# A mixture-of-experts stage: expert sums as 64-token transposes on two half arrays, gate temporaries in SBUF, and a later order of preparation

## The chip, the cores and the metric

The kernel runs on one core of one Trainium2 chip. The metric is the device time of one execution in microseconds (us); the median of three runs is 1518.93 us (1518.44 to 1519.48).

## The reference

The input has shape 16 x 64 x 36 x 100 (batch, channels, height, width), float32. Cut to what matters:

```python
x = x + conv(ln_c(x), w_d, w_u, w_r, w_l)       # four recurrent sweeps: down, up, right, left
t = to_tokens(x)                                # 57600 tokens of 64 channels
probs = softmax(ln_t(t) @ router_w + router_b)  # 8 experts
top_p, top_i = top_k(probs, 2); top_p /= sum(top_p)
expert_out = einsum('bnd,edc->bnec', ln_t(t), expert_w) + expert_b
t = t + einsum('bnk,bnkc->bnc', top_p, take(expert_out, top_i))
```

So every token goes through all eight 64 x 64 experts, and the gate, which is zero for six of them, weights the eight results before they are summed.

## The kernel before

The program has three stages: the vertical sweeps, row by row; the horizontal sweeps, column by column; and, from about 920 us on, the feed-forward stage, which is all that the change touches. In that stage the image lies in SBUF as 18 regions `j` of 128 partitions x 1600 positions (two image rows share the partitions, 64 channels each). A region is cut into 13 tiles `p` of 128 positions, the last of 64, and a tile's two halves `q` (the two image rows) are 2 x 128 tokens. Tiles are taken three at a time as five chunks `c` for the preparation.

While a region's experts run, the next region is prepared between them. Every engine has its instructions in an order written out by hand in its own `region` function, loop over `p`:

- TensorE (PE): `experts(p)`, six matmuls of 512 columns in two halves of 64 rows, the tile's tokens against all experts into one of two twin banks; `tokens(c)`, centring and router logits (L977); `channels(c)`, transposes back (L991); `sum_experts(p-2)`, four accumulating transposes of a 128 x 128 block (L1022), which add the eight weighted results and turn them into the image's layout.
- VectorE (DVE): `gate_tile(p)` (L793) weights the experts' results, both halves of a tile (1024 elements) or one half (512); `square_sums` (L725), `second_part` (L733), the 17 steps of the gate's softmax and top two (L749 to L765, at places that `STEP_AT` names as (tile, part)), and `add_out` (L801), which adds the sums of four tiles to the image.
- ScalarE (ACT): `gate_odd(p)` (L506) weights the other half of the tiles in `ACT_TILES`, eight instructions each; `copy_tokens` (L473, L474), `inv_std_tokens` (L481, L483), `first_part` (L491).
- GpSimd (POOL): `pair_sums(p)` (L322) adds experts 4 to 7 to experts 0 to 3, so that four blocks are left; `scale_tokens(c)` (L335, L336) at tiles 2 to 6, ahead of that tile's pair sums.

`experts(p)` waits until both gate engines are through with tile p-2. `channels(c)` waits for `second_part(c-1)`, since both use bank 5. The sum of a group of four tiles waits until `add_out` has read the group before from bank 7 (`SUM`). Softmax step 0 waits for the last `scale_tokens` of the region, later steps each for the one before. Its temporaries `work` and `small` and the bias row lie in PSUM bank 6 (`LOG`).

Of the kernel before, what the change touches and what calls it, by code (L numbers as in the profile page):

```python
# [12 lines left out]
def metaformer_kernel(nc, x, x_col, w_d, w_u, w_r, w_l, router_w, router_b, expert_w, expert_b, out):  # L13
# [13 lines left out]
    TN = 128  # L27
# [10 lines left out]
    with ctx:  # L38
# [69 lines left out]
        CEN0, VAR0 = [2, 3, 6, 7], [4, 5]  # L108
        FRONT = CH + 2
        CT, TB = 4, 5  # L110
        LOG, SUM = 6, 7
        PREP = [6, 7]
        FILL_CT, FILL_TB = [4, 0, 1, 2, 3], [5, 7, 5, 7, 5]

        ACT_TILES = (2, 4, 5, 6, 7, 8, 9, 10)
        TERMS = [(0, 0), (0, 1), (1, 0)]
        LAG = 2
        SEQ = 2 * TILES
# [4 lines left out]

            return len(ACT_TILES) * j + sum(a <= p for a in ACT_TILES)

        bias_row = banks[LOG][:, 2 * NSM + 3 * NG:2 * NSM + 3 * NG + E]

        def stage_of(k):

# [16 lines left out]
        def later(n):  # L146
# [5 lines left out]
        GAP_STEP = 8  # L152
        EX_STEP = 12

        STEP_AT = [(7, 0), (7, 1), (7, 2), (8, 0), (8, 1), (8, 2), (9, 0), (9, 1), (9, 2), (10, 0), (10, 1), (10, 2),
                   (11, 0), (11, 1), (11, 2), (12, 0), (12, 1)]
        EXP_TILE = STEP_AT[GAP_STEP - 1][0] + 1

# [196 lines left out]
        def _(act):  # L355
# [109 lines left out]
            def copy_tokens(j, slot, c, bank=CT):  # L465
                n, b, k = NCK * j + c, (slot + c) % 2, len(tiles_of(c))
                src = banks[bank][:, 0:TC * CLW].rearrange("p (t n) -> p t n", t=TC)[:, 0:k]
                act.wait_ge(s_ct, n + 1)
                if later(n - 1):
                    act.wait_ge(s_vr, n - 1)  # L470
                if later(j):
                    act.wait_ge(s_tb, n - NCK + 1)
                act.activation(sqt[:, b, 0:k], src[:, :, 0:P], ACT.Square).then_inc(s_sq2, 1)  # L473
                act.activation(tl[:, c, 0:k], src, ACT.Copy).then_inc(s_cp, 1)  # L474

            def inv_std_tokens(j, slot, c):
                n, b, k = NCK * j + c, (slot + c) % 2, len(tiles_of(c))
                act.wait_ge(s_vr, n + 1)
                if later(n - 1):
                    act.wait_ge(s_xn2, n - 1)  # L480
                act.activation(stat[:, 1, b, 0:2 * k], stat[:, 0, b, 0:2 * k], ACT.Ln, bias=eps_c[:, 1:2], scale=1.0 / C).then_inc(s_ln2, 1)  # L481
                act.wait_ge(s_ln2, n + 1)
                act.activation(stat[:, 2, b, 0:2 * k], stat[:, 1, b, 0:2 * k], ACT.Exp, scale=-0.5).then_inc(s_r2, 1)  # L483

            def first_part(j, slot, c, bank=TB):

                n, k = NCK * j + c, len(tiles_of(c))
                act.wait_ge(s_tb, n + 1)
                if c == 0 and later(j - 1):
                    act.wait_ge(s_p, TILES * (j - 1))  # L490
                act.activation(tok[:, slot, 0, TC * TN * c:TC * TN * c + TN * k], banks[bank][:, 0:TN * k],  # L491
                               ACT.Identity, bias=1.0).then_inc(s_th, 1)
# [17 lines left out]
            def region(j, slot, now):  # L510

                for p in range(TILES):
                    if now is not None:
                        if p == EXP_TILE:
                            exponential(now)
                        if 2 <= p < NCK + 2:
                            inv_std_tokens(now, 1 - slot, p - 2)
                    if p in ACT_TILES:
                        gate_odd(j, slot, p)
                    if now is not None:  # L520
                        if p < NCK:
                            copy_tokens(now, 1 - slot, p)
                        if 3 <= p < NCK + 3:
                            first_part(now, 1 - slot, p - 3)

            for c in range(NCK + 2):
                if c < NCK:
# [15 lines left out]
        def _(dve):  # L543
# [96 lines left out]
            for q in range(2):  # L640
                half = slice(q * C, (q + 1) * C)
                nc.vector.tensor_copy(cl_w[half, P + q * E:P + (q + 1) * E], ew[half, E * C:]).then_inc(s_em, 1)
            nc.vector.tensor_copy(bias_row, eb[:, E * C:]).then_inc(s_em, 1)
            dve.wait_ge(s_em, 8)
            nc.vector.tensor_tensor(em[:, 1], ew[:, 0:E * C], em[:, 0].bitcast(F32), ALU.subtract).then_inc(s_em, 1)
            with dve.Fori(1, (HP - 2) // 2) as i:
# [70 lines left out]
            def flat(j):  # L717
                return cols[:, j].rearrange("p g w b -> p (g w b)")
# [18 lines left out]
                return v.unsqueeze(2).to_broadcast([P, NG, E])  # L737

            gap, ex, inv = (best[:, k] for k in range(3))
            work = banks[LOG][:, 0:2 * NSM].rearrange("p (k n e) -> p k n e", k=2, e=E)  # L740
            small = banks[LOG][:, 2 * NSM:2 * NSM + 3 * NG].rearrange("p (k n) -> p k n", k=3)
            m1, idx, den = (small[:, k] for k in range(3))

            def softmax_steps(j, slot):


                v = nc.vector
                return [
                    lambda: v.tensor_tensor(logit, raw_logit, bias_row.unsqueeze(1).to_broadcast([P, NG, E]), ALU.add),  # L749
                    lambda: v.tensor_reduce(m1, logit, AX.X, ALU.max),  # L750
                    lambda: v.tensor_tensor(work[:, 0], logit, spread(m1), ALU.subtract),
                    lambda: v.scalar_tensor_tensor(hit, work[:, 0], 0.0, rank_w[:, :, :], ALU.is_equal, ALU.mult),
                    lambda: v.tensor_reduce(idx, hit, AX.X, ALU.max),
                    lambda: v.tensor_tensor(first, rank_w[:, :, :], spread(idx), ALU.is_equal),
                    lambda: v.scalar_tensor_tensor(work[:, 1], first, -BIG, work[:, 0], ALU.mult, ALU.add),
                    lambda: v.tensor_reduce(gap, work[:, 1], AX.X, ALU.max),
                    lambda: v.tensor_tensor(work[:, 1], work[:, 1], spread(gap), ALU.subtract),
                    lambda: v.scalar_tensor_tensor(hit, work[:, 1], 0.0, rank_w[:, :, :], ALU.is_equal, ALU.mult),
                    lambda: v.tensor_reduce(idx, hit, AX.X, ALU.max),
                    lambda: v.tensor_tensor(work[:, 0], rank_w[:, :, :], spread(idx), ALU.is_equal),  # L760
                    lambda: v.tensor_scalar(den, ex, 1.0, None, ALU.add),
                    lambda: v.reciprocal(inv, den),
                    lambda: v.tensor_tensor(work[:, 1], work[:, 0], spread(ex), ALU.mult),
                    lambda: v.tensor_tensor(work[:, 0], work[:, 1], first, ALU.add),
                    lambda: v.tensor_tensor(gate[slot], work[:, 0], spread(inv), ALU.mult),  # L765
                ]
# [28 lines left out]
            def add_out(j, g):  # L795

                lo, hi = g * QUAD, min((g + 1) * QUAD, TILES)
                width, off = (QUAD * TN, 0) if hi < TILES else (TAIL, TN - TAIL)
                dst = flat(j)[:, lo * TN:lo * TN + width]
                dve.wait_ge(s_y, TILES * j + hi)  # L800
                nc.vector.tensor_tensor(dst, banks[SUM][:, off:off + width], dst, ALU.add).then_inc(s_o, 1)  # L801

            def add_behind(j, p):

# [7 lines left out]
            def region(j, slot, now):  # L812

                for p in range(TILES):
                    for part in range(3):
                        if part == 0:
                            gate_tile(j, slot, p)
                            if now is not None:
                                if 1 <= p < NCK + 1:
                                    square_sums(now, 1 - slot, p - 1)  # L820
                                if 4 <= p < NCK + 4:
                                    second_part(now, 1 - slot, p - 4)
                        if part == 2:
                            add_behind(j, p)
                        if now is not None:
                            softmax(now, 1 - slot, (p, part))
# [21 lines left out]
        def _(pe):  # L848
# [165 lines left out]
            def sum_experts(j, slot, p):  # L1014

                n = TILES * j + p
                pe.wait_ge(s_ps, n + 1)
                if p % QUAD == 0:
                    pe.wait_ge(s_o, GROUPS * j + p // QUAD + 2)
                at = (p % QUAD) * TN  # L1020
                for e in range(E // 2):
                    last = mm(banks[SUM][:, at:at + TN], stage(slot, p)[:, e], ident[:, :],  # L1022
                              start=e == 0, stop=e == E // 2 - 1, is_transpose=True)
                last.then_inc(s_y, 1)

            def region(j, slot, now):
                for p in range(TILES):
                    experts(j, slot, p)
                    if now is not None:
                        if p < NCK:  # L1030
                            tokens(now, 1 - slot, p)
                        if 3 <= p < NCK + 3:
                            channels(now, 1 - slot, p - 3)
                    if p >= LAG:
                        sum_experts(j, slot, p - LAG)
                    elif later(j):
                        sum_experts(j - 1, 1 - slot, TILES + p - LAG)
# [83 lines left out]
```

## Time and profile before

| | |
|---|---|
| median of 3 runs | 1518.93 us |
| the profiled execution, its own time | 1521.44 us |
| its span in the trace | 1519.7 us |
| PE busy | 1351.9 us, 89% |
| DVE busy | 842.6 us, 55% |
| ACT busy | 708.9 us, 47% |
| POOL busy | 630.5 us, 41% |
| chain that ended last | PE 75%, DVE 11%, issue 7%, ACT 4% |

Busy shares are means over three stages with different limits, so the feed-forward stage is read by itself. PE's matmuls are pipelined and overlap in the records; the distance between starts tells more than their length. "Idle before" is the time an engine stood still just before an instruction, with what ended it.

### The profile page before, as it was taken

The numbers are of one execution on the slowest core, as the hardware profiler recorded it, in microseconds if no ns is written. First come the engines' busy times: TensorE is split into PE (matmuls) and PEld (weight loads), VectorE is DVE, ScalarE is ACT, GpSimd is POOL, SyncE is SP. The second block draws the span as 40 slices with busy tenths as digits, with TensorE's granted clock in tenths as the row PEclk, the third lists the DMA queues.
The fourth block names the chain that finished last, engine by engine and source line by source line (L and its number), as shares of the span: only waits on it lengthen the run. The fifth ranks groups of instructions, "written<-read, shape, count | busy, mean of one in ns | idle before, by whom it ended". The sixth has DMA issues, their size and how long they took to land.

```text
span 1519.7 us, 30382 instructions
## 1 busy us (share of the span) xinstructions
PE 1351.9 (89%) x9344; PEld 1181.8 (78%) x9344; DVE 842.6 (55%) x1786; ACT 708.9 (47%) x2313; POOL 630.5 (41%) x752
## 2 busy tenths in 40 slices
PE   7899999999998999999999997777777777777777
PEld 5899999999998999999999995445555445555544
DVE  4788888555552222222222225667776667776666
ACT  5567766334342222220000004666666666667664
POOL 2566665000000000003444444666666666666666
PEclk9999999999999999999999997999999999999999
DMA  4111111000000000001121110000001000000001
GB/s 135 44 65 47 61 65 61 1 0 0 0 0 0 0 0 0 0 0 39 58 77 59 58 58 1 22 23 23 22 24 42 22 22 22 22 30 36 23 23 44
DMA packets 15372, 46.68 MB, mean 31 GB/s; under 512 B 2912, under 2 KB 2912, under 8 KB 15328
## 3 DMA queue, kind: packets, MB, share of 16 engines
q1 hardware_dynamic: 15184, 45.76, 8.5%
q8 instruction: 28, 0.46, 0.1%
q10 hardware_dynamic: 144, 0.33, 0.1%
q14 instruction: 16, 0.13, 0.0%
HBM read 31.33 MB, written 14.75 MB: 30 GB/s over the span
## 4 chain that ended last, share of the span: by engine, by line
PE 75%; DVE 11%; issue 7%; ACT 4%; DVEq 1%; POOL 1%; DMA 0%; ACTq 0%; POOLq 0%
PE twin L954 30%; PE twin L871 24%; PE twin L1010 8%; PE twin L1022 5%; DVE parts L733 3%; PE twin L991 3%; PE twin L977 2%; PE twin L862 2%; PE twin L856 2%; DVE scratch L793 1%; DVE stat L725 1%; DVE act_buf L801 1%; ACT more L506 1%; ACT late L506 1%; DVE late L793 1%
## 5 line engine op out<-in xcount | busy, mean ns | idle before, releaser
L954 PE MATMUL twin<-kbuf,late 128*128 128x136 f32 (+2 forms) x3940 | 458.1, 280 | 5.0 <-DVE kbuf L701 5.0
L954 PEld LDWEIGHTS twin<-kbuf,late 128*128 128x128 f32 x3940 | 457.9, 192 | 5.3 <-DVE kbuf L701 5.3
L871 PE MATMUL twin<-parts 128*128 128x384 f32 (+2 forms) x2070 | 393.8, 342 | 0.0
L871 PEld LDWEIGHTS twin<-parts 128*128 128x128 f32 x2070 | 372.5, 189 | 2.9 <-issue 2.5
L297 POOL TENSOR_TENSOR act_buf<-kbuf,x_in 128x144 f32 (+1 forms) x198 | 96.6, 488 | 564.7 <-DVE kbuf L707 564.7
L707 DVE SCALAR_TENSOR_TENSOR kbuf<-twin,act_buf 128x144 f32<-128x144 f32 x394 | 121.3, 308 | 337.1 <-PE twin L954 337.1
L1010 PE MATMUL twin<-em,parts 64*128 64x512 f32 x1404 | 228.7, 431 | 2.8 <-DVE scratch L793 2.8
L322 POOL TENSOR_TENSOR scratch<-scratch 128x512 f32<-128x512 f32 x126 | 160.8, 1276 | 112.4 <-ACT scratch L506 73.5
L473 ACT ACTIVATE x_in<-twin 128x384 f32<-128x384 f32 (+1 forms) x90 | 42.0, 467 | 336.0 <-PE twin L977 336.0
L793 DVE TENSOR_TENSOR scratch<-twin,scratch 128x512 f32<-128x512 f32 (+1 forms) x126 | 115.5, 917 | 95.0 <-PE twin L1010 91.1
L1010 PEld LDWEIGHTS twin<-em,parts 64*128 64x128 f32 x1404 | 115.1, 187 | 52.8 <-issue 38.9
L459 ACT ACTIVATE act_buf<-kbuf 128x144 f32 x196 | 63.2, 323 | 167.3 <-DVE kbuf L707 167.3
L506 ACT ACTIVATE scratch<-twin,scratch 128x64 f32<-128x64 f32 x576 | 124.6, 340 | 30.4 <-PE twin L1010 30.3
L991 PE MATMUL twin<-ident,x_in 128*128 128x128 f32 x234 | 43.3, 286 | 100.8 <-DVE parts L733 97.1
L991 PEld LDWEIGHTS twin<-ident,x_in 128*128 128x128 f32 x234 | 26.4, 143 | 126.2 <-POOL x_in L336 92.5
L977 PEld LDWEIGHTS twin<-cl_w,act_buf 128*128 128x128 f32 x468 | 63.5, 194 | 49.2 <-ACT x_in L474 27.1
L322 POOL TENSOR_TENSOR late<-late 128x512 f32<-128x512 f32 x63 | 80.3, 1275 | 45.6 <-ACT late L506 35.7
L1022 PE MATMUL twin<-ident,scratch 128*128 128x128 f32 x504 | 78.6, 279 | 23.1 <-DVE act_buf L801 22.3
L279 POOL TENSOR_TENSOR x_parts<-x_in,eps_c 128x400 fp32r<-128x400 f32 x66 | 56.3, 853 | 101.7 <-PE twin L856 81.6
L977 PE MATMUL twin<-cl_w,act_buf 128*128 128x144 f32 x468 | 82.3, 310 | 15.6 <-ACT x_in L474 13.6
L281 POOL TENSOR_TENSOR x_parts<-x_in,x_parts 128x400 fp32r<-128x400 f32 x66 | 92.9, 1408 | 5.2
L1022 PEld LDWEIGHTS twin<-ident,scratch 128*128 128x128 f32 x504 | 56.9, 141 | 43.8 <-POOL scratch L322 31.9
(102 smaller groups left out, 1585.2 us busy)
## 6 DMA issues: line engine op xcount, KB each, us to landing
x_in<-x SPq DMA_DIRECT2D x36, 400.0 KB, 3.6
x_in<-x_col SPq DMA_DIRECT2D x20, 720.0 KB, 4.1
result<-act_buf SPq DMA_DIRECT2D x36, 400.0 KB, 2.8
scratch<-L_conv_w_d ACTq DMA_DIRECT2D x1, 320.0 KB, 4.7
scratch<-L_conv_w_u SPq DMA_DIRECT2D x1, 320.0 KB, 6.0
late<-L_conv_w_r SPq DMA_DIRECT2D x1, 320.0 KB, 6.3
late<-L_conv_w_l SPq DMA_DIRECT2D x1, 320.0 KB, 7.0
ew<-L_ffn_expert_w SPq DMA_DIRECT2D x2, 128.0 KB, 6.2
```

Source lines behind the costliest of these rows:

```text
L281: nc.gpsimd.tensor_tensor(x_parts[:, b, 1], src, x_parts[:, b, 0].bitcast(F32), ALU.subtract).then_inc(s_xp, 1)
L297: nc.gpsimd.tensor_tensor(cols[:, :, g, w], kbuf[:, g], x_blk[:, slot, i, g], ALU.add).then_inc(s_cb[g], 1)
L322: nc.gpsimd.tensor_tensor(buf[:, 0:4], buf[:, 0:4], buf[:, 4:8], ALU.add).then_inc(s_ps, 1)
L506: last = act.activation(stage(slot, p)[:, e, C:P], twin[(TILES * slot + p) % 2][:, 1, e * C:(e + 1) * C], ACT.Copy, scale=gate[slot][:, 2 ...
L707: nc.vector.scalar_tensor_tensor(kbuf[:, g], banks[CONV[g]][:, 0:NH].rearrange("p (j b) -> p j b", j=HP), 0.0, cols[:, :, g, w], ALU.max, ...
L793: nc.vector.tensor_tensor(dst, src, scl, ALU.mult).then_inc(s_g, 1)
L871: last = mm(acc[:, lo:hi], vw[:, k, wpart, si], carry[:, cpart, g, lo + s * BG:hi + s * BG], start=first and si == 0, stop=final and si == ...
L954: last = mm(banks[CONV[g]][:, lo * BG:hi * BG], hw[:, k, si], kbuf[:, g, lo + s:hi + s].rearrange("p j b -> p (j b)"), start=si == 0, stop ...
L977: last = mm(banks[bank][:, CLW * i:CLW * (i + 1)], flat[:, tile_lo(p):tile_lo(p) + TN], cl_w[:, :], start=True, stop=True)
L991: last = mm(banks[bank][:, TN * i:TN * (i + 1)], tl[:, c, i, 0:P], ident[:, :], start=True, stop=True, is_transpose=True)
L1010: last = mm(twin[(TILES * slot + p) % 2][:, q, 0:E * C], tok[half, slot, l, span], em[half, b], start=k == 0, stop=k == len(TERMS) - 1)
L1022: last = mm(banks[SUM][:, at:at + TN], stage(slot, p)[:, e], ident[:, :], start=e == 0, stop=e == E // 2 - 1, is_transpose=True)
```

## The change

The sum of a tile becomes eight transposes: for each of four blocks, tokens 0 to 63 on the upper half array into bank 6 and tokens 64 to 127 on the lower one into bank 7, with 64 moving columns each; `add_out` reads both banks in one instruction. Bank 6 is no longer free, so the softmax's temporaries go to SBUF (in `sq`, unused in this stage) and the bias row to an SBUF tensor. The order changes on all engines: `channels` and its two followers from tile c+3 (DVE c+4 for `second_part`) to c+5, `inv_std_tokens` from c+2 to c+1, softmax step 0 from (7, 0) to (6, 2) with the steps behind it up to one place earlier, and `ACT_TILES` from eight tiles to seven, 6 to 12. POOL's own order is the same.

```diff
-        LOG, SUM = 6, 7
+        SUMS = [6, 7]
-        ACT_TILES = (2, 4, 5, 6, 7, 8, 9, 10)
+        ACT_TILES = (6, 7, 8, 9, 10, 11, 12)
-        bias_row = banks[LOG][:, 2 * NSM + 3 * NG:2 * NSM + 3 * NG + E]
+        bias_row = sb("bias_row", [P, E])
-        STEP_AT = [(7, 0), (7, 1), (7, 2), (8, 0), (8, 1), (8, 2), (9, 0), (9, 1), (9, 2), (10, 0), (10, 1), (10, 2),
+        STEP_AT = [(6, 2), (7, 0), (7, 1), (7, 2), (8, 0), (8, 1), (8, 2), (9, 0), (9, 2), (10, 0), (10, 1), (10, 2),
                    (11, 0), (11, 1), (11, 2), (12, 0), (12, 1)]
...
-                        if 2 <= p < NCK + 2:
-                            inv_std_tokens(now, 1 - slot, p - 2)
+                        if 5 <= p < NCK + 5:
+                            first_part(now, 1 - slot, p - 5)
+                        if p < NCK:
+                            copy_tokens(now, 1 - slot, p)
                     if p in ACT_TILES:
                         gate_odd(j, slot, p)
-                    if now is not None:
-                        if p < NCK:
-                            copy_tokens(now, 1 - slot, p)
-                        if 3 <= p < NCK + 3:
-                            first_part(now, 1 - slot, p - 3)
+                    if now is not None and 1 <= p < NCK + 1:
+                        inv_std_tokens(now, 1 - slot, p - 1)
...
-            work = banks[LOG][:, 0:2 * NSM].rearrange("p (k n e) -> p k n e", k=2, e=E)
-            small = banks[LOG][:, 2 * NSM:2 * NSM + 3 * NG].rearrange("p (k n) -> p k n", k=3)
+            spare = sq[:, :, :].rearrange("p b n -> p (b n)")
+            work = spare[:, 0:2 * NSM].rearrange("p (k n e) -> p k n e", k=2, e=E)
+            small = spare[:, 2 * NSM:2 * NSM + 3 * NG].rearrange("p (k n) -> p k n", k=3)
...
-                width, off = (QUAD * TN, 0) if hi < TILES else (TAIL, TN - TAIL)
-                dst = flat(j)[:, lo * TN:lo * TN + width]
+                width, first_half = (QUAD * TN, 0) if hi < TILES else (TAIL, 2 - TAIL // C)
+                dst = flat(j)[:, lo * TN:lo * TN + width].rearrange("p (t r n) -> p r t n", r=2 - first_half, n=C)
+                src = twin[SUMS[0] // 2][:, first_half:, 0:(hi - lo) * C].rearrange("p r (t n) -> p r t n", n=C)
                 dve.wait_ge(s_y, TILES * j + hi)
-                nc.vector.tensor_tensor(dst, banks[SUM][:, off:off + width], dst, ALU.add).then_inc(s_o, 1)
+                nc.vector.tensor_tensor(dst, src, dst, ALU.add).then_inc(s_o, 1)
...
+                    if now is not None and 1 <= p < NCK + 1:
+                        square_sums(now, 1 - slot, p - 1)
+                    gate_tile(j, slot, p)
+                    if now is not None and 5 <= p < NCK + 5:
+                        second_part(now, 1 - slot, p - 5)
                     for part in range(3):
-                        if part == 0:
-                            gate_tile(j, slot, p)
-                            if now is not None:
-                                if 1 <= p < NCK + 1:
-                                    square_sums(now, 1 - slot, p - 1)
-                                if 4 <= p < NCK + 4:
-                                    second_part(now, 1 - slot, p - 4)
...
-                at = (p % QUAD) * TN
+                at = (p % QUAD) * C
                 for e in range(E // 2):
-                    last = mm(banks[SUM][:, at:at + TN], stage(slot, p)[:, e], ident[:, :],
-                              start=e == 0, stop=e == E // 2 - 1, is_transpose=True)
+                    for r in range(2):
+                        half = slice(r * C, (r + 1) * C)
+                        last = mm(banks[SUMS[r]][:, at:at + C], stage(slot, p)[half, e], ident[half, half],
+                                  start=e == 0, stop=e == E // 2 - 1, is_transpose=True)
...
+                        if 5 <= p < NCK + 5:
+                            channels(now, 1 - slot, p - 5)
                         if p < NCK:
                             tokens(now, 1 - slot, p)
-                        if 3 <= p < NCK + 3:
-                            channels(now, 1 - slot, p - 3)
```

The first place is PE at tiles 3 and 4 of a region in the middle of the program. Before (L1010 is `experts`, L977 `tokens`, L991 `channels`, L1022 the sum):

```order
L1010 MATMUL twin<-em,parts 128x512 [waits s_g,s_tl]
L977 MATMUL twin<-cl_w,act_buf 128x144 [waits s_cp]
L991 MATMUL twin<-ident,x_in 128x128 [waits s_tl,s_xn2]
L1022 MATMUL twin<-ident,late 128x128 [waits s_ps]
L1022 MATMUL twin<-ident,late 128x128 x3
L1010 MATMUL twin<-em,parts 128x512 [waits s_ga,s_g]
```

With the change, tiles 4 and 5 (L1009 is `experts`, L976 `tokens`, L990 `channels`, L1023 the sum):

```order
L1009 MATMUL twin<-em,parts 128x512 [waits s_g]
L976 MATMUL twin<-cl_w,act_buf 128x144 [waits s_cp]
L1023 MATMUL twin<-ident,more 128x64 [waits s_ps]
L1023 MATMUL twin<-ident,more 128x64 x7
L1009 MATMUL twin<-em,parts 128x512 [waits s_g]
L990 MATMUL twin<-ident,x_in 128x128 [waits s_tl,s_xn2]
L1023 MATMUL twin<-ident,scratch 128x64 [waits s_ps]
L1023 MATMUL twin<-ident,scratch 128x64 x7
```

The transposes back no longer share a tile with `tokens`; they stand in tiles 5 to 9, one tile behind the DVE instruction that they wait for. The sum has eight matmuls of 64 columns where it had four of 128.

The second place is DVE at tiles 6 and 7. Before (L793 is the gate, L733 `second_part`, L749 softmax step 0, and so on):

```order
L793 TENSOR_TENSOR scratch<-twin,scratch 128x8x64 [waits s_p]
L733 SCALAR_TENSOR_TENSOR parts<-twin,parts 128x384 [waits s_th]
L749 TENSOR_TENSOR scratch<-scratch,twin 128x208 [waits s_xn2]
L750 TENSOR_REDUCE twin<-scratch 128x26 [waits s_sm]
L751 TENSOR_TENSOR twin<-scratch,twin 128x208 [waits s_sm]
L752 SCALAR_TENSOR_TENSOR scratch<-twin,rank_w 128x208 [waits s_sm]
```

With the change (L732 is `second_part`):

```order
L793 TENSOR_TENSOR more<-twin,scratch 128x8x64 [waits s_p]
L732 SCALAR_TENSOR_TENSOR parts<-twin,parts 128x384 [waits s_th]
L749 TENSOR_TENSOR scratch<-scratch,bias_row 128x208 [waits s_xn2]
L793 TENSOR_TENSOR scratch<-twin,scratch 128x8x64 [waits s_p]
L750 TENSOR_REDUCE sq<-scratch 128x26 [waits s_sm]
L751 TENSOR_TENSOR sq<-scratch,sq 128x208 [waits s_sm]
L752 SCALAR_TENSOR_TENSOR scratch<-sq,rank_w 128x208 [waits s_sm]
```

Step 0 now stands ahead of the gate of tile 7, and its wait for `s_xn2` (POOL's last scaling) with it. Steps that read one operand from PSUM (`twin`) now read both from SBUF.

## Rows read from the trace of the kernel before

**Rows 1.** Busy time by window, mid-stage: us, busy and count per engine, PEclk, DMA.

```profile
1200.00:1300.00 100.00, 76.50 (x525) 51.41 (x525) 70.83 (x135) 66.88 (x274) 65.48 (x71) 1.00 0.06 25
```

**Rows 2.** Timeline of PE: start, us, instruction, [idle before <-releaser]. Tiles 1 to 3, 9.

```profile
1202.49 0.97 PE L1010 MATMUL twin<-em,parts 64*128 64x512 f32 x6
...
1204.76 0.96 PE L1010 MATMUL twin<-em,parts 64*128 64x512 f32 x6
...
1208.27 0.96 PE L1010 MATMUL twin<-em,parts 64*128 64x512 f32 x6
...
1211.04 0.52 PE L991 MATMUL twin<-ident,x_in 128*128 128x128 f32 x3 [1.36 <-DVE parts L733]
...
1222.97 0.98 PE L1010 MATMUL twin<-em,parts 64*128 64x512 f32 x6
...
1224.46 0.97 PE L1010 MATMUL twin<-em,parts 64*128 64x512 f32 x6
```

**Rows 3.** Timeline of DVE over one region, from one tile 0 to the next.

```profile
1199.96 1.23 DVE L793 TENSOR_TENSOR scratch<-twin,scratch 128x1024 f32<-128x1024 f32 x1 [0.23 <-PE twin L1022]
1201.10 0.68 DVE L801 TENSOR_TENSOR act_buf<-twin,act_buf 128x512 f32 x1
...
1202.83 0.54 DVE L725 TENSOR_REDUCE stat<-x_in 128x6 f32<-128x384 f32 x1
1203.29 0.21 DVE L801 TENSOR_TENSOR act_buf<-twin,act_buf 128x64 f32 x1
1203.51 0.69 DVE L793 TENSOR_TENSOR late<-twin,scratch 128x512 f32<-128x512 f32 x1
...
1220.12 0.55 DVE L733 SCALAR_TENSOR_TENSOR parts<-twin,parts 128x384 fp32r<-128x384 f32 x1
1220.58 0.36 DVE L749 TENSOR_TENSOR scratch<-scratch,twin 128x208 f32<-128x208 f32 x1
1220.97 0.38 DVE L750 TENSOR_REDUCE twin<-scratch 128x26 f32<-128x208 f32 x1
...
1232.47 1.23 DVE L793 TENSOR_TENSOR scratch<-twin,scratch 128x1024 f32<-128x1024 f32 x1 [0.31 <-PE twin L1022]
```

**Rows 4.** Timeline of POOL in the same region, tiles 1, 2 and 6.

```profile
1202.99 1.28 POOL L322 TENSOR_TENSOR scratch<-scratch 128x512 f32<-128x512 f32 x1 [0.46 <-DVE scratch L793]
1204.22 0.27 POOL L335 TENSOR_TENSOR scratch<-x_in,stat 128x48 f32<-128x48 f32 x1
1204.45 0.83 POOL L336 TENSOR_TENSOR x_in<-x_in,stat 128x384 f32<-128x384 f32 x1
...
1216.20 0.40 POOL L336 TENSOR_TENSOR x_in<-x_in,stat 128x128 f32<-128x128 f32 x1
```

**Rows 5.** Timeline of ACT: the odd halves of two tiles.

```profile
1222.49 3.38 ACT L506 ACTIVATE scratch<-twin,scratch 128x64 f32<-128x64 f32 x16 [1.06 <-PE twin L1010]
```

**Rows 6.** First stage, line L281: count, duration ns min/median/max, start.

```profile
L281 POOL TENSOR_TENSOR x_parts<-x_in,x_parts x66: 1027/1440/1495, 21.5 to 256.1; 128x400 fp32r<-128x400 f32 x66
```

**Rows 7.** Timelines of DVE and of POOL, first stage, around 203.5 us.

```profile
203.51 0.57 DVE L617 TENSOR_TENSOR parts<-sq,parts 128x400 fp32r<-128x400 f32 x1 [0.60 <-ACT sq L363]
...
203.56 1.44 POOL L281 TENSOR_TENSOR x_parts<-x_in,x_parts 128x400 fp32r<-128x400 f32 x1
```

**Rows 8.** DVE's line L571 (durations of both), and POOL's timeline there.

```profile
L571 DVE TENSOR_TENSOR parts<-scratch,parts x2: 826/916/1005, 6.3 to 57.2; 128x640 fp32r<-128x640 f32 x2
...
56.66 0.85 POOL L279 TENSOR_TENSOR x_parts<-x_in,eps_c 128x400 fp32r<-128x400 f32 x1 [2.12 <-PE twin L856]
```

**Rows 9.** The stage's beginning: busy time by window, and PE's timeline.

```profile
940.00:945.00 5.00, 4.80 (x20) 3.62 (x22) 2.89 (x5) 3.17 (x14) 4.43 (x5) 0.50 0.00 0
...
940.20 1.65 PE L1010 MATMUL twin<-em,parts 64*128 64x512 f32 x6 [2.76 <-DVE scratch L793]
...
944.37 1.22 PE L1010 MATMUL twin<-em,parts 64*128 64x512 f32 x4
```

More of the change, by code:

```diff
@@ L642, in _ @@
                 nc.vector.tensor_copy(cl_w[half, P + q * E:P + (q + 1) * E], ew[half, E * C:]).then_inc(s_em, 1)
-            nc.vector.tensor_copy(bias_row, eb[:, E * C:]).then_inc(s_em, 1)
+            nc.vector.tensor_copy(bias_row[:, :], eb[:, E * C:]).then_inc(s_em, 1)
             dve.wait_ge(s_em, 8)
@@ L748, in softmax_steps @@
                 return [
-                    lambda: v.tensor_tensor(logit, raw_logit, bias_row.unsqueeze(1).to_broadcast([P, NG, E]), ALU.add),
+                    lambda: v.tensor_tensor(logit, raw_logit, bias_row[:, :].unsqueeze(1).to_broadcast([P, NG, E]), ALU.add),
                     lambda: v.tensor_reduce(m1, logit, AX.X, ALU.max),
```

## The prediction

> **What bounds the kernel now.** I read the busy time by window first, since only the feed-forward stage changes. In its middle no engine is full: of 100 us PE is busy 76.5, DVE 70.8, ACT 66.9, POOL 65.5, at the full granted clock [rows 1]. So a region is bounded by waits, and the timelines tell which. The gate of tile 0 starts on DVE at 1199.96 and again at 1232.47 [rows 3]: one region takes 32.5 us, and 17 regions carry the preparation of a next one.
>
> PE's timeline shows three kinds of tile. With `tokens` and no wait a tile takes 1204.76 - 1202.49 = 2.27 us; with experts and sum alone 1224.46 - 1222.97 = 1.49. In a tile with `channels` PE starts the experts at 1208.27, and the transposes back only at 1211.04, 1.36 us idle before them, ended by DVE's `second_part` [rows 2]. That is a ring inside one tile: experts, then DVE's gate, square sums and `second_part`, then the transposes, then the next experts. It stands in five tiles of each region, and is worth about 5 x 1.4 = 7 us of it.
>
> **The change, part by part.**
>
> *Transposes back at c+5.* DVE's `second_part(c-1)` is then in the tile ahead of `channels(c)`, so the ring of 7 us a region is gone. What is late next is worked out below.
>
> *The sum.* The four transposes of 128 columns are what the experts leave of a tile of 1.49 us; their records are 0.98 long and overlap what follows a little, so 0.5 to 0.6 us with the change of array shape [rows 2]. Eight of 64 columns cost between half of that (if the two halves run side by side, each pair in the time of 64 columns) and nearly twice that (if each takes as long as a present one), so 0.25 to 0.9 us a tile. I take 0.3, since the experts are the nearest row: 64 partitions each, six matmuls of 512 columns in 0.98 us, which one after the other would need more than twice the 0.52 us that three full-height transposes take for 384 columns. PE has room: at 2.1 to 2.7 us a tile with `tokens` it stays level with or not far from POOL's 2.27 (below), and it starts a region 3 to 4 us ahead of the gates. Both ends give the same region time.
>
> *ACT.* Sixteen of its instructions take 3.38 us [rows 5], so a tile's odd half 1.6. One tile fewer: 1.6 us off ACT, 0.5 onto DVE (the double gate holds DVE for 1.14 us, to the start of what follows, the single one 0.61 [rows 3]). DVE's work in a region becomes 6 x 1.14 + 7 x 0.61 for gates, 2.0 for square sums, 2.0 for `second_part`, 17 softmax steps at 0.39 or less, 2.0 for adding out: 23.5 us. It is the fullest engine, and 32.5 could fall to about that if nothing else held it.
>
> *POOL's stretch.* Something else does. Softmax step 0 waits for the last scaling, and now stands ahead of tile 7's gate. Count from the start of tile 0's gate on DVE. The gate of tile 1 ends at 1.14 + 0.60 (add out) + 0.46 + 1.22 = 3.4. From there POOL never waits: pair sums hold it 1.23 us, a scaling 0.23 + 0.83 with 0.04 overlapped [rows 4], so 2.27 a tile; four of these, one more pair sum, and the small scaling, 0.57, make 10.9. The last scaling ends at 14.4. DVE was through with tile 6's `second_part` at about 11.9 and stands still for 2.5 us.
>
> *The temporaries in SBUF.* Eleven of the 17 steps (L749, L751, L752, L754, L755, L757, L758, L760, L763, L764, L765) now have both inputs in SBUF; before none had. What such an instruction does beside POOL is seen in the first stage. POOL's L281 takes 1.03 us alone and 1.44 in the median [rows 6], where DVE's L617, two SBUF inputs, starts just ahead of it [rows 7]: POOL loses 0.41, about the time of L617's 400 elements. The other way round there is one row: L571 takes 0.83 us alone, and 1.01 at 57.2, where POOL's L279 had been running since 56.66 and ended at 57.51 [rows 8]. DVE lost 0.18 of the 0.3 us left of it, POOL nothing. So whoever starts first keeps the other out until nearly its end. POOL's pair sum takes 1.28 us, so it holds DVE out for up to 1.2; a softmax step holds POOL out for 0.2.
>
> From 14.4 on I follow both engines. POOL's pair sum of tile p starts at the end of both gates of tile p, or when POOL is free; its hold ends 0.1 before its end. Seven steps meet one (step: DVE ready, hold ends):
> L749: 14.4, 15.5 (POOL goes straight from the scaling into tile 6). L751: 17.3, 17.8. L754: 20.0, 21.0 (this pair sum waits for ACT, whose gate of tile 8 stands behind `first_part`, which waits for the transposes behind `second_part` of tile 7). L757: 23.6, 23.7. L760: 25.5, 26.2. L763: 27.7, 28.5. L765: 29.9, 31.0. Between them DVE does what stands in its order at the times above, with steps at 0.40 (0.36 to 0.38 and a restart [rows 3]). The waits sum to 5.3 us, and the next tile 0 starts at 31.3. PE and ACT are never later than this: the experts of the next tile 0 can start at 27.3.
>
> The region: 32.5 - 31.3 = 1.2 us less. So 7 us of stall are removed, and nearly all comes back, 2.5 as DVE's wait for the last scaling, 5.3 as holds, less what DVE had idle at other places.
>
> The Trainium skill, "SBUF — State Buffer", section "Who interferes with whom", calls the port pair that DVE and GpSimd share an exclusive lock: the loser fully blocks. By that rule the region is the 31.3 above. If instead the single row of L571 is taken as a fixed loss of 0.18 per meeting, it is 31.3 - 5.3 + 7 x 0.18 = 27.3. I take the first, since 0.18 of 0.3 is most of what was left of a shorter instruction.
>
> *Clock.* In each region PE would now stand still for 2 to 3 us twice (tiles 8 and 10). At 940.20, after 2.76 us idle, the records show it at half clock, 1.2 GHz, in the window 940 to 945, where experts take 1.65 us and a `tokens` tile 4.17 [rows 9]. I expect some such falls, mostly inside PE's room of 3 us: 0.15 us a region, between 0 and 4 (below).
>
> *Ends.* In the last region no next one is prepared, and six tiles without ACT go at POOL's 1.28 instead of some at 1.6: 2 us less. First sweeps and loads: nothing changes.
>
> **The sum.** 17 x (1.2 - 0.15) + 2 = 20 us. Against the profiled execution's span, 1519.7, that gives 1499.7; its own time, 1521.44, lies 2.5 above the median of the runs, so I set the 20 against the median: 1518.9 - 20 = **1499 us**. My following of the ring may be off by 0.2 us at each of seven meetings, 1.3 us a region, so 1477 to 1521 for this case.
>
> **The rivals.**
>
> *A, DVE is not held* (chance 0.20). Only POOL pays, 0.2 us a step, in gaps that it has. Then from 14.4 on DVE works without a pause, 16.9 - 5.3 = 11.6 us, and the region is 26.0: 1518.9 - 17 x 6.5 - 2 = 1406; with the fixed loss of 0.18, 17 x 5.2 less, 1429. For it: a single row speaks for the hold, and there DVE's loss was small. Against it: POOL's 60-odd rows of L281 show that the port is not shared in halves.
>
> *B, the holds meet less often* (0.07). DVE gets in ahead of POOL at half of the meetings: 28.7 us a region, 1518.9 - 17 x 3.8 - 2 = 1452.
>
> *C, the clock, slower* (0.11). If PE runs at half clock through the `tokens` tiles, each takes 4.17 instead of 2.27 us. POOL's stretch needs the gate of tile 5 by 11.8, which leaves PE some 3.4 us of room; five slow tiles add 8.3, so the region gets 4.9 longer than 31.3, 36.2: 1518.9 + 17 x 3.7 - 2 = 1580. It decides from where slow tiles use up the room and the gain of 1.2, 4.6 / 1.9 = 2.4 slow tiles a region. For it: the fall at 940 after an idle stretch as long as those that I expect. Against it: PE's work falls in the busy tiles 0 to 5, not behind the long idle stretches, and in the middle of the stage the clock held 1.00 with PE idle a quarter of the time [rows 1].
>
> The skill's "TensorE: Matmul & The Clock Gate", part 4, says that transposes do not engage the full clock. By that the sum's eight small transposes would count for nothing and C would be likelier. The trace does not bear it out: more than a third of a tile of 1.49 us is transposes [rows 2], and the clock stood at 1.00 [rows 1].
>
> *D, the half arrays do not run side by side.* The sum then costs 0.9 us a tile. `tokens` tiles take 2.7, and PE's room covers it: still 1499. It changes no chance.
>
> **How the numbers follow.** The forecast has 0.62, of which 0.04 end above and 0.03 within 0.2% of before, 3 us, which is what a measurement of this kernel can tell. Faster: 0.55 + 0.20 + 0.07 = 0.82; same 0.03; slower 0.04 + 0.11 = 0.15. The range takes in the forecast's own, B, and the upper half of A: 1418 to 1524 leaves out a tenth below and a tenth above.
>
> **What the profile would show.** If right: regions of 31.3 us; no idle time before L990 worth the name; DVE idle 2 us or more before L749, ended by POOL; and softmax steps with two SBUF inputs that take 0.37 us in some tiles and up to 1.5 in others (L749, L754, L760, L763 and L765 longest), while L750, L753, L756, L759 stay at 0.38. If A holds, all of these stay under 0.6 and DVE is busy 90% of a region. If C holds, PEclk is clearly under 1.0 from 950 on. The forecast is wrong if the wait before L749 is missing, or if POOL's pair sums rather than DVE's steps get long.

## The result, and the profile after

The changed kernel takes 1474.81 us (median of four runs, 1473.68 to 1477.92), 44 us less than before: ratio 0.971, 95% interval 0.970 to 0.972. The forecast was 1499, 20 us less. The direction and the kinds of wait were right; the gain was more than twice the forecast.

The busy time by window in the middle of the stage, with the columns of [rows 1] (us, then PE, PEld, DVE, ACT, POOL busy, PEclk, DMA):

```profile
1200.00:1300.00 100.00, 81.69 (x733) 56.95 (x735) 91.61 (x147) 65.53 (x263) 68.64 (x74) 0.86 0.07 26
```

DVE is busy 91.6% instead of 70.8% [rows 1], and the granted clock is 0.86 instead of 1.00. The waits, longest in total, from 1010 to 1450 us (who waited for whom: us, times, longest):

```profile
PE twin L1023 <- DVE act_buf L802: 31.7, 23, 2.0
PE twin L990 <- DVE parts L732: 31.7, 33, 2.0
DVE scratch L749 <- POOL x_in L336: 21.2, 14, 1.9
```

Over the same stretch of the kernel before, PE waited 79 us for `second_part`; now it is 32 (and as much for `add_out`, where it was 17). In its place DVE stands still ahead of softmax step 0 until POOL's last scaling. The timelines of DVE and POOL over the region from 1205.08 to 1234.78 show both halves of the forecast. DVE:

```profile
1205.08 1.23 DVE L793 TENSOR_TENSOR scratch<-twin,scratch 128x1024 f32<-128x1024 f32 x1 [0.23 <-DVE scratch L765]
...
1216.97 0.56 DVE L732 SCALAR_TENSOR_TENSOR parts<-twin,parts 128x384 fp32r<-128x384 f32 x1
1219.41 1.43 DVE L749 TENSOR_TENSOR scratch<-scratch,bias_row 128x208 f32<-128x208 f32 x1 [1.88 <-POOL x_in L336]
1220.77 0.68 DVE L793 TENSOR_TENSOR scratch<-twin,scratch 128x512 f32<-128x512 f32 x1
...
1221.84 0.35 DVE L750 TENSOR_REDUCE sq<-scratch 128x26 f32<-128x208 f32 x1
1222.22 0.89 DVE L751 TENSOR_TENSOR sq<-scratch,sq 128x208 f32<-128x208 f32 x1
1223.15 0.37 DVE L752 SCALAR_TENSOR_TENSOR scratch<-sq,rank_w 128x208 f32<-128x208 f32 x1
...
1224.90 1.42 DVE L754 TENSOR_TENSOR scratch<-rank_w,sq 128x208 f32<-128x208 f32 x1
...
1228.32 0.67 DVE L757 TENSOR_TENSOR sq<-sq,best 128x208 f32<-128x208 f32 x1
...
1230.31 1.00 DVE L760 TENSOR_TENSOR sq<-rank_w,sq 128x208 f32<-128x208 f32 x1
...
1232.39 0.37 DVE L763 TENSOR_TENSOR sq<-sq,best 128x208 f32<-128x208 f32 x1
...
1233.28 0.85 DVE L764 TENSOR_TENSOR sq<-sq,scratch 128x208 f32<-128x208 f32 x1
1234.17 0.37 DVE L765 TENSOR_TENSOR scratch<-sq,best 128x208 f32<-128x208 f32 x1
1234.78 1.23 DVE L793 TENSOR_TENSOR scratch<-twin,scratch 128x1024 f32<-128x1024 f32 x1 [0.23 <-DVE scratch L765]
```

POOL:

```profile
1208.57 1.27 POOL L322 TENSOR_TENSOR late<-late 128x512 f32<-128x512 f32 x1 [0.92 <-DVE late L793]
...
1218.98 0.40 POOL L336 TENSOR_TENSOR x_in<-x_in,stat 128x128 f32<-128x128 f32 x1
1219.34 1.27 POOL L322 TENSOR_TENSOR more<-more 128x512 f32<-128x512 f32 x1
1221.61 1.27 POOL L322 TENSOR_TENSOR scratch<-scratch 128x512 f32<-128x512 f32 x1 [0.99 <-DVE scratch L793]
1224.82 1.27 POOL L322 TENSOR_TENSOR scratch<-scratch 128x512 f32<-128x512 f32 x1 [1.94 <-ACT scratch L506]
...
1232.49 1.41 POOL L322 TENSOR_TENSOR scratch<-scratch 128x512 f32<-128x512 f32 x1 [1.41 <-ACT scratch L506]
1234.31 1.38 POOL L322 TENSOR_TENSOR late<-late 128x512 f32<-128x512 f32 x1 [0.40 <-ACT late L506]
```

Read them side by side. The pair sum of tile 1 starts 3.5 us into the region, the last scaling ends at 1219.38, 14.3 us into it, and step 0 follows. But the pair sum of tile 6 started at 1219.34, 0.07 ahead of it, and the 0.37 us step takes 1.43. It happens again at 1222.22 and at 1224.90, where POOL had started at 1221.61 and 1224.82. Reductions (L750), with one SBUF input, stay at 0.35, and POOL's own 1.27 is unchanged in these three. The last two pair sums show the other direction: L763 and L765 had started 0.10 and 0.14 us ahead of them and keep their 0.37, and it is POOL that takes 1.41 and 1.38. The region takes 29.7 us instead of 32.5 [rows 3].

### The profile page after: what moved, and what is told of

Read it like the earlier page. It is cut to its first block, busy times and chain, and to the rows that moved or that the text cites. A ratio compares the mean times of both kernels' runs of the same rounds, so it can differ in the third digit from the quotient of the medians.

```text
span 1471.3 us, 32041 instructions
## 1 busy us (share of the span) xinstructions
PE 1344.4 (91%) x10280; PEld 1184.1 (80%) x10280; DVE 917.6 (62%) x1786; ACT 677.2 (46%) x2169; POOL 629.9 (43%) x752
## 4 chain that ended last, share of the span: by engine, by line
PE 72%; DVE 11%; issue 9%; POOL 4%; ACT 3%; DVEq 0%; DMA 0%; POOLq 0%; ACTq 0%
PE twin L953 31%; PE twin L870 25%; PE twin L1009 6%; PE twin L976 4%; PE twin L1023 3%; PE twin L861 2%; PE twin L855 2%; DVE parts L732 2%; POOL x_in L336 2%; DVE scratch L793 1%; POOL scratch L322 1%; DVE scratch L765 1%; DVE act_buf L802 1%; DVE scratch L754 1%; DVE sq L751 1%
## 5 line engine op out<-in xcount | busy, mean ns | idle before, releaser
L1009 PE MATMUL twin<-em,parts 64*128 64x512 f32 x1404 | 259.5, 477 | 8.7 <-DVE scratch L793 3.5
L1009 PEld LDWEIGHTS twin<-em,parts 64*128 64x128 f32 x1404 | 142.6, 221 | 23.0 <-issue 8.6
L793 DVE TENSOR_TENSOR scratch<-twin,scratch 128x512 f32<-128x512 f32 (+1 forms) x126 | 119.9, 952 | 9.6 <-PE twin L1009 4.5
L506 ACT ACTIVATE scratch<-twin,scratch 128x64 f32<-128x64 f32 x504 | 112.4, 394 | 5.5 <-PE twin L1009 5.3
L1023 PEld LDWEIGHTS twin<-ident,scratch 64*128 64x128 f32 x1008 | 50.4, 157 | 72.7 <-issue 41.1
L1023 PE MATMUL twin<-ident,scratch 64*128 64x64 f32 x1008 | 65.2, 255 | 39.2 <-DVE act_buf L802 30.0
L976 PEld LDWEIGHTS twin<-cl_w,act_buf 128*128 128x128 f32 x468 | 66.7, 202 | 37.2 <-ACT x_in L474 20.9
L281 POOL TENSOR_TENSOR x_parts<-x_in,x_parts 128x400 fp32r<-128x400 f32 x66 | 93.0, 1409 | 5.2
L976 PE MATMUL twin<-cl_w,act_buf 128*128 128x144 f32 x468 | 85.9, 320 | 2.2 <-POOL act_buf L314 2.0
L990 PEld LDWEIGHTS twin<-ident,x_in 128*128 128x128 f32 x234 | 26.9, 150 | 75.3 <-issue 61.0
L431 ACT ACTIVATE parts<-scratch 128x400 fp32r<-128x400 f32 x68 | 36.6, 538 | 106.7 <-DVE scratch L656 106.7
```

Of the source, the lines that this page charges most:

```text
L281: nc.gpsimd.tensor_tensor(x_parts[:, b, 1], src, x_parts[:, b, 0].bitcast(F32), ALU.subtract).then_inc(s_xp, 1)
L506: last = act.activation(stage(slot, p)[:, e, C:P], twin[(TILES * slot + p) % 2][:, 1, e * C:(e + 1) * C], ACT.Copy, scale=gate[slot][:, 2 ...
L793: nc.vector.tensor_tensor(dst, src, scl, ALU.mult).then_inc(s_g, 1)
L976: last = mm(banks[bank][:, CLW * i:CLW * (i + 1)], flat[:, tile_lo(p):tile_lo(p) + TN], cl_w[:, :], start=True, stop=True)
L1009: last = mm(twin[(TILES * slot + p) % 2][:, q, 0:E * C], tok[half, slot, l, span], em[half, b], start=k == 0, stop=k == len(TERMS) - 1)
L1023: last = mm(banks[SUMS[r]][:, at:at + C], stage(slot, p)[half, e], ident[half, half], start=e == 0, stop=e == E // 2 - 1, is_transpose=True)
```

## The experiments

All times stand beside 1518.8 to 1519.3 us for the kernel before on the same chip.

**order_alone and one_bank.** Two kernels without DVE steps that read twice from SBUF. `order_alone` is the kernel before with only the new order; the sum and bank 6 are as before. `one_bank` has the whole change except the place of the temporaries. With the new order `tokens` (tiles 0 to 4) and `channels` (tiles 5 to 9) no longer overlap in time, so one bank does for both:

```diff
-        CT, TB = 4, 5
-        SUMS = [6, 7]
+        CT, TB = 7, 7
+        LOG, SUMS = 6, [4, 5]
...
-            spare = sq[:, :, :].rearrange("p b n -> p (b n)")
...
+            work = banks[LOG][:, 0:2 * NSM].rearrange("p (k n e) -> p k n e", k=2, e=E)
...
+                if c == 0 and later(j):
+                    pe.wait_ge(s_tl, NCK * j)
...
+                if c == 0 and later(j):
+                    pe.wait_ge(s_cp, NCK * (j + 1))
```

> The kernel before with the new order only: four transposes of 128 columns into bank 7, temporaries in bank 6. Theory: the ring of channels is gone and nothing takes its place but DVE's wait for the last scaling; region 25.7 to 26.7, time 1405 to 1425, so the split sum and the move of the temporaries together cost some 50 to 70 us of what the order gives. Rival (the split sum matters, since PE with old sums is too slow in the tiles with tokens): region above 28, time above 1445.

> The changed kernel with tokens and channels in one PSUM bank (7; they no longer overlap in time), the sums in banks 4 and 5, and so bank 6 free again for the softmax's temporaries and the bias row. No DVE step has two SBUF inputs. Theory (the holds by POOL's pair sums are paid in full by DVE, 4.2 us a region in the changed kernel's trace): every softmax step is 0.38 us or less, the part of a region from step 0 on shrinks from 15.4 to about 11.4 us, the region from 29.8 to 25.7, the time to about 1405 us. The 1.9 us that DVE waits for POOL's last scaling stay. Rival (the holds lie in time that DVE would wait anyway, for ACT or PE): the steps are short, but DVE waits for PE at the gates instead, and the time stays above 1455.

Measured: `order_alone` 1410.3 us (ratio 0.929, 0.927 to 0.930), `one_bank` 1404.7 (0.925, 0.923 to 0.926). DVE's timeline of one_bank, one region (here L792 is the gate, L748 step 0):

```profile
1208.60 0.56 DVE L732 SCALAR_TENSOR_TENSOR parts<-twin,parts 128x384 fp32r<-128x384 f32 x1
1210.69 0.37 DVE L748 TENSOR_TENSOR scratch<-scratch,twin 128x208 f32<-128x208 f32 x1 [1.54 <-POOL x_in L336]
...
1214.62 0.37 DVE L753 TENSOR_TENSOR scratch<-rank_w,twin 128x208 f32<-128x208 f32 x1
...
1222.12 1.23 DVE L792 TENSOR_TENSOR scratch<-twin,scratch 128x1024 f32<-128x1024 f32 x1 [0.31 <-DVE scratch L764]
```

The wait ahead of step 0 is still there, 1.54 us; every step takes 0.38 or less, though 116 of them start while a pair sum runs; and from step 0 to the next region it is 11.4 us instead of 15.4. `order_alone` came inside its range, 1405 to 1425, and `one_bank` within 1 us of its 1405. Added in this sequence, the change is three parts: the order gives 108.5 us, the split sum (with the shared bank and its two waits) 5.5 more, and the temporaries in SBUF take 70 back. The parts depend on the sequence: the runs below have the last two in the old order.

**temps_alone.** The kernel before with only the temporaries and the bias row in SBUF:

```diff
-        bias_row = banks[LOG][:, 2 * NSM + 3 * NG:2 * NSM + 3 * NG + E]
+        bias_row = sb("bias_row", [P, E])
...
-            work = banks[LOG][:, 0:2 * NSM].rearrange("p (k n e) -> p k n e", k=2, e=E)
-            small = banks[LOG][:, 2 * NSM:2 * NSM + 3 * NG].rearrange("p (k n) -> p k n", k=3)
+            spare = sq[:, :, :].rearrange("p b n -> p (b n)")
+            work = spare[:, 0:2 * NSM].rearrange("p (k n e) -> p k n e", k=2, e=E)
+            small = spare[:, 2 * NSM:2 * NSM + 3 * NG].rearrange("p (k n) -> p k n", k=3)
```

> The kernel before with only the temporaries and the bias row in SBUF. Theory: from step 0 on DVE works without a pause in the kernel before (11.9 us), so holds there are paid: six or seven meetings, 2 to 4 us a region, time 1550 to 1585. The first step meets none, since POOL has no scaling right ahead of it. Rival (the slack of 9.7 us of DVE idle in a region takes the holds in): time within 10 us of 1519.

Measured: 1586.4 us (ratio 1.044, 1.043 to 1.046), 68 slower than before, 1.4 above the expectation's range. Its lines for the steps L752, L755, L761 and L766 (duration ns min/median/max), and for a reduction between them:

```profile
L752 DVE TENSOR_TENSOR sq<-scratch,sq x18: 375/1464/1469, 932.3 to 1542.6; 128x208 f32<-128x208 f32 x18
L754 DVE TENSOR_REDUCE sq<-scratch x18: 369/370/372, 933.1 to 1544.9; 128x26 f32<-128x208 f32 x18
L755 DVE TENSOR_TENSOR scratch<-rank_w,sq x18: 374/1457/1466, 933.5 to 1545.3; 128x208 f32<-128x208 f32 x18
L761 DVE TENSOR_TENSOR sq<-rank_w,sq x18: 374/1212/1221, 935.9 to 1550.1; 128x208 f32<-128x208 f32 x18
L766 DVE TENSOR_TENSOR scratch<-sq,best x18: 374/1340/1348, 937.8 to 1555.2; 128x208 f32<-128x208 f32 x18
```

The same instruction on the same shape takes 0.37 us when POOL is idle (the first region's preparation, the minimum) and up to 1.47 beside a pair sum. In most regions five meetings of 0.7 to 1.1 us and a small one make 4.8 us, and a region takes 36.4 us instead of 32.5, 3.9 more. DVE's idle time takes in less than 1 us of the holds: of its 9.7 us a region in the kernel before, 8.6 lie ahead of step 0, and the holds behind it. So the rival fell.

**old_order and old_order_sum_twice.** `old_order` adds the split sum to temps_alone. The second does every sum twice over, into the same columns:

```diff
-                for e in range(E // 2):
+                for e in [*range(E // 2), *range(E // 2)]:
```

> Split sum and temporaries in SBUF, in the order of before. Against temps_alone it shows what the split sum gives by itself. Theory: the sum lies in PE's ring in the five tiles with channels and in the tiles behind them, 0.25 to 0.5 us a tile, so 2 to 3 us a region less than temps_alone, 1515 to 1545. Rival (the sum is off the path): the same as temps_alone within 5 us.

> old_order with every sum done twice over (the eight transposes of a tile again, into the same columns, the second time overwriting the first; the result is the same). Theory (the split sum is slower in the old order only because it leaves PE idle for more of the time, so that its clock is granted at 0.78 instead of 0.95 to 1.00 and the ring through channels runs at half clock): more work brings the clock back above 0.9, and the time falls to 1580 to 1600. Rival (two banks, eight instructions or the half arrays cost by themselves): twice the sums cost 0.25 us a tile more on the path, time 1610 to 1660.

`old_order` took 1606.6 us (1.058, 1.057 to 1.060), 20 slower than temps_alone. Both expectations of it were wrong: the theory had it faster, the rival the same within 5 us. The windows from 1100 to 1300 us of temps_alone, of old_order and of old_order_sum_twice give the clue, each in a fence:

```profile
1100.00:1300.00 200.00, 141.99 (x929) 94.11 (x928) 152.31 (x246) 120.11 (x496) 115.91 (x124) 0.97 0.05 21
```

```profile
1100.00:1300.00 200.00, 143.47 (x1158) 100.22 (x1156) 141.19 (x231) 118.46 (x482) 112.86 (x123) 0.78 0.06 21
```

```profile
1100.00:1300.00 200.00, 143.28 (x1806) 108.19 (x1802) 150.68 (x247) 119.11 (x489) 116.97 (x122) 0.96 0.06 22
```

The clock (PEclk, the last but two) is 0.97, 0.78 and 0.96. The split sum needs PE for less time, the old order leaves PE waiting about 1.4 us in every tile with `channels`, and the clock goes to its lower level, 1.2 GHz. PE's timeline of old_order, in that ring:

```profile
1255.87 0.87 PE L993 MATMUL twin<-ident,x_in 128*128 128x128 f32 x3 [1.35 <-DVE parts L733]
1256.67 0.69 PE L1026 MATMUL twin<-ident,scratch 64*128 64x64 f32 x8
1257.12 1.63 PE L1012 MATMUL twin<-em,parts 64*128 64x512 f32 x6
1260.09 0.45 PE L993 MATMUL twin<-ident,x_in 128*128 128x128 f32 x1 [1.34 <-DVE parts L733]
```

and the ring in old_order_sum_twice, one tile earlier in its region:

```profile
1204.70 0.52 PE L993 MATMUL twin<-ident,x_in 128*128 128x128 f32 x3 [1.54 <-DVE parts L733]
1205.15 0.71 PE L1026 MATMUL twin<-ident,scratch 64*128 64x64 f32 x16
1205.67 0.94 PE L1012 MATMUL twin<-em,parts 64*128 64x512 f32 x6
1207.96 0.52 PE L993 MATMUL twin<-ident,x_in 128*128 128x128 f32 x3 [1.34 <-DVE parts L733]
```

From one group of transposes back to the next it is 4.22 us with 8 matmuls a sum and 3.26 with 16 (3.27 to the group after). `old_order` has the comparison in itself, too: in three of its regions these tiles ran at the full clock, with groups at 1215.84 and 1218.85, 3.01 us apart, and such a region takes 35.9 us, less than temps_alone's 36.4; the others take 37.1 or more. The time with the sums doubled is 1583.4 us (1.043, 1.041 to 1.045): 23 us less for more work. The expectation of the clock theory, 1580 to 1600, held; that two banks or eight instructions cost by themselves is refuted.

**after_sum_twice.** The same edit to the changed kernel, whose clock was 0.86.

> The changed kernel with every sum done twice over, as in old_order_sum_twice. The changed kernel's clock was 0.83 to 0.94 a region. Theory (PE is off the path of a region there, which runs over POOL's stretch and DVE's held steps): the clock rises above 0.9 and the time stays within 10 us of 1475. Rival (part of the changed kernel's time is the low clock): the time falls by 15 us or more, as it did by 23 in the old order.

Measured: 1470.6 us (0.969, 0.967 to 0.970), clock from 1100 to 1300 us at 0.96. The expectation held, 4 us less. But this is a net figure and no bound on what the low clock costs, since the doubled sums cost time themselves: step 0 comes 14.7 us into a region in the mean instead of 14.4, while the holds shrink from 4.1 us a region to 3.3. So PE isn't wholly off the path: when it runs decides which steps meet a pair sum. How the 4 us divide is not shown.

**one_bank_steps_late, steps_late, late_act8, late_sum_twice.** What is left to gain. The first two put the softmax steps back to the places of before, in one_bank and in the changed kernel:

```diff
-        STEP_AT = [(6, 2), (7, 0), (7, 1), (7, 2), (8, 0), (8, 1), (8, 2), (9, 0), (9, 2), (10, 0), (10, 1), (10, 2),
+        STEP_AT = [(7, 0), (7, 1), (7, 2), (8, 0), (8, 1), (8, 2), (9, 0), (9, 1), (9, 2), (10, 0), (10, 1), (10, 2),
```

> one_bank with the softmax steps at the places of before: step 0 at (7, 0), behind the gate and the second part of tile 7. Theory (after the holds, what is left to gain is DVE's 1.6 us of idle time ahead of step 0, ended by POOL's last scaling): both instructions, 1.1 us, slip into the wait; region 24.6 to 24.8 instead of 25.75, time 1385 to 1390. Rival (the gate of tile 7 waits for PE just as long): DVE idles ahead of the gate instead, time within 4 us of 1405.

> The changed kernel with the softmax steps at the places of before, temporaries still in SBUF. Theory: the wait ahead of step 0 shrinks by about 1.1 us a region, but the holds stay, 3 to 5 us a region; time 1445 to 1470. If the holds depended on where a step stands and mostly went away, it would be under 1430.

Measured: 1400.2 us (0.922, 0.920 to 0.923) and 1460.7 (0.961, 0.959 to 0.963). The second is as expected. The first gained 4.5 us where 15 to 20 were expected. DVE's timeline of one_bank_steps_late shows why:

```profile
1180.72 0.56 DVE L732 SCALAR_TENSOR_TENSOR parts<-twin,parts 128x384 fp32r<-128x384 f32 x1 [0.56 <-ACT parts L491]
1181.20 0.36 DVE L748 TENSOR_TENSOR scratch<-scratch,twin 128x208 f32<-128x208 f32 x1
```

DVE is no longer idle ahead of L748, but the instruction pulled in front of it, `second_part`, waits for ACT, which stands in the gate of tile 6. The rival named PE; it is ACT, with the same effect. In that kernel DVE is busy 183.4 of 200 us, so little is left on this engine.

Two edits to one_bank_steps_late. `late_act8` gives tile 5 to ACT as well, `late_sum_twice` does every sum twice, by the same edit as in old_order_sum_twice:

```diff
-        ACT_TILES = (6, 7, 8, 9, 10, 11, 12)
+        ACT_TILES = (5, 6, 7, 8, 9, 10, 11, 12)
```

> one_bank_steps_late with tile 5 given to ACT as well (eight tiles). Theory: DVE is the fullest engine and loses 0.5 us of work a region; region 24.2, time about 1378. Rival: ACT's odd half of tile 5 comes behind its first part of chunk 0, so POOL's pair sum of tile 5 and the last scaling start later, and the time is 1385 to 1400.

> one_bank_steps_late with every sum done twice over. Every second region there had the clock at 0.93 and a part behind step 0 of 10.9 us where the others had 10.5. Theory: the clock stays at 1.00 and those regions lose 0.4 us, but 0.25 us a tile more work on a PE that is 90% busy takes it back; 1395 to 1410. Rival (the clock is worth more than the work): under 1395, the fastest version.

Measured: 1407.4 us (0.927, 0.925 to 0.928) and 1422.6 (0.937, 0.935 to 0.938), 7 and 22 slower than without; both lie above everything that was expected of them. In `late_act8` the work taken off DVE came back as a wait, but not the rival's: the last scaling still ends 14.3 us into a region, and it is `second_part` that waits longer for ACT, 21.4 us between 1010 and 1300 instead of 6.1. In `late_sum_twice` DVE's gates wait for PE, 17.5 us in the same stretch instead of 5.7: this kernel has no long idle time of PE to spend, as the old order had.

The fastest kernel of this study is one_bank_steps_late, 1400.2 us, ahead of the changed kernel by 5% and of the kernel before by 7.8%.

## Why the prediction came out as it did

- *The ring of channels goes* (7 us a region). Right. With only DVE's wait for the last scaling in its place, in one_bank, a region takes 25.8 us instead of 32.5.
- *POOL's stretch and DVE's wait for the last scaling.* Right, and sized well: 14.3 us from the gate of tile 0 to step 0, forecast 14.4. DVE's idle time ahead of it is 1.9 us in that region, not 2.5.
- *DVE is held out by POOL's pair sums.* Right in kind, shown by the steps' durations and by three kernels. The forecast's exclusive lock ("Who interferes with whom" in the Trainium skill's "SBUF — State Buffer") is borne out: a step of 0.37 us takes up to 1.50 beside a 1.28 us pair sum, so it waits 1.1. Rival A, in which only POOL pays, had a fifth of the chance and is refuted; its region of 26.0 us is what one_bank shows once no step reads twice from SBUF.
- *"The waits sum to 5.3 us, and the next tile 0 starts at 31.3."* This is the step that failed, in its size. The region above has 1.06 on L749, 0.52 on L751, 1.05 on L754, 0.30 on L757, 0.63 on L760 and 0.49 on L764: 4.05 us. Over the 17 regions the steps' durations above 0.36 to 0.38 come to between 3.1 and 5.5 us, 4.1 in the mean. Up to L760 the meetings were as forecast in this region; the forecast then had L763 and L765 held for 0.8 and 1.1, and here it is L764 for 0.5. I had followed POOL's pair sums of tiles 10 to 12 as if they started at the end of DVE's gate. They start when ACT's half is done too, and "PE and ACT are never later than this" was wrong: ACT's gate of tile 11 waits for PE. ACT's timeline of the changed kernel:

```profile
1227.98 1.75 ACT L506 ACTIVATE scratch<-twin,scratch 128x64 f32<-128x64 f32 x8
1230.66 1.75 ACT L506 ACTIVATE scratch<-twin,scratch 128x64 f32<-128x64 f32 x8 [0.93 <-PE twin L1009]
```

  The experts that it waits for ran at the lower clock. PE's timeline there, with one tile from before the fall:

```profile
1219.17 0.94 PE L1009 MATMUL twin<-em,parts 64*128 64x512 f32 x6
1222.06 0.52 PE L990 MATMUL twin<-ident,x_in 128*128 128x128 f32 x3 [1.95 <-DVE parts L732]
...
1228.97 1.66 PE L1009 MATMUL twin<-em,parts 64*128 64x512 f32 x6
```

  Behind 1.95 us of idle time, and 0.78 and 1.36 more, the experts take 1.66 us instead of 0.94. With the 0.7 us less ACT would have waited some 0.2 (an estimate from these rows), so in this region most of the slip of the pair sum of tile 11 comes from the clock, which the forecast had kept apart from the holds.

  A pair sum that starts later can meet another step, or an instruction that it doesn't hold: here L763 got in 0.10 us ahead of it and L765 0.14 us ahead of the next one. In other regions (from 1176.09, for one) the pair sum of tile 6 starts only 0.6 us after the scaling, again behind ACT, and L749 takes 0.37.
- *The sum over regions.* From the first tile 0 to that of the last region it is 507.7 us, 17 x 29.87. The forecast was 31.3 + 0.15. The difference of 1.6 us a region is 1.2 from the holds, and the rest from DVE's own work behind step 0 (11.3 us instead of 11.6) and the term for the clock. Seventeen times 1.6 is 27 us. The 2 us forecast for the last region did not come (from its tile 0 to the end it is 27.8 us, before 27.5), and 27 less 2 is 25, against the 24 that the forecast was short.
- *The clock.* It fell more than expected, to between 0.77 and 0.94 a region. The forecast had 2.5 us for it; what it cost is not shown, since it also moved the pair sums (above), and doubling the sums gave 4 us net. Rival C did not happen in this kernel: the low clock lies in tiles 9 to 12, and the `tokens` tiles ran at full clock in the region above. A fall of the clock that lengthens a kernel showed itself in old_order.
- *Rival D.* The half arrays do run side by side: records of PE in the changed kernel give 0.46 to 0.47 us for eight overlapping transposes at full clock. The split sum gives 5.5 us of 1410; that it is so little because PE has room there is argued, not shown.
- The time lay inside the range because the range covered the kernels without holds too. The forecast's own range, 1477 to 1521, missed it by 2 us.

## What to carry to other kernels

Count, before moving a VectorE temporary from PSUM to SBUF, which of its instructions will then read SBUF twice, and what GpSimd runs beside them: each meeting cost up to 1.1 us for a 0.37 us step, and of DVE's 9.7 us of idle time a region less than 1 covered it. When a new order frees a bank's lifetime, look for two users that no longer overlap in time before giving the bank's other tenant up; that was worth 70 us here. Where PE waits a lot, read the granted clock beside every time: less work on PE made this kernel slower in its old order. When adding up waits that depend on which instruction starts first, follow every engine that releases one of them; 0.1 us decided here whether a step was held.

## What was not expected of the hardware

- Less PE work, longer time: with the split sum in the old order the mean granted clock fell from 0.97 to 0.78 and the time rose by 20 us; doing each sum twice brought 0.96 back and took 23 us off. The work that was added is transposes alone. The same doubling gave 4 us in the changed kernel and cost 22 in one_bank_steps_late.
- Eight transposes of 64 x 64 on two half arrays, behind others of their kind, start in pairs about 0.06 us apart, where full 128 x 128 ones start 0.11 apart in the kernel before; sixteen take 0.71 us in the records, eight 0.46.
- Whichever engine starts first keeps its time: a VectorE step with two SBUF inputs that starts behind a pair sum takes up to 1.50 us instead of 0.37, and a pair sum that starts behind such a step up to 1.50 instead of 1.28. In one_bank, whose steps read one input from PSUM, 116 steps start inside a pair sum and none takes over 0.38.
